# Layer 0 of a four-layer gated cross-attention stack: another path for every second softmax unit

## The reference, cut to what matters

```
q = (emb @ Wq.T).reshape(B, SQ, 16, 64).transpose(0, 2, 1, 3)
k = (context @ Wk.T).reshape(B, SK, 16, 64).transpose(0, 2, 1, 3)
v = (context @ Wv.T).reshape(B, SK, 16, 64).transpose(0, 2, 1, 3)
q = _layernorm(q, qn_w, qn_b)
k = _layernorm(k, kn_w, kn_b)
attn = jnp.einsum('bhqd,bhkd->bhqk', q, k) * scale
attn = jax.nn.softmax(attn, axis=-1)
out = jnp.einsum('bhqk,bhkd->bhqd', attn, v)
return out.reshape(B, SQ, 16 * 64) @ Wu.T + bu      # heads gathered first
x = x + jnp.tanh(g_xattn[0]) * out
```

## Time and profile before

| | |
|---|---|
| median of 3 runs | 1539.65 us (1536.65 to 1540.21) |
| the profiled execution, timed | 1535.79 us |
| its span, first to last instruction | 1533.6 us |
| TensorE busy | 1393.0 us, 91% |
| VectorE busy | 805.6 us, 53% |
| ScalarE busy | 756.1 us, 49% |
| GpSimd busy | 124.2 us, 8% |
| mean granted TensorE clock | 0.978 of full speed |

### The profile page before, as it was taken

How to read it: one execution, slowest core, us unless ns; L and a number is a source line. 1 busy time by engine, 2 the same in 40 slices (tenths; PEclk the granted TensorE clock), 3 DMA queues, 4 the chain that set the end, 5 groups by cost and what they waited for, 6 DMA issues and landing times.

```text
span 1533.6 us, 26446 instructions
## 1 busy us (share of the span) xinstructions
PE 1393.0 (91%) x8788; PEld 1129.2 (74%) x8788; DVE 805.6 (53%) x2147; ACT 756.1 (49%) x1622; POOL 124.2 (8%) x115
## 2 busy tenths in 40 slices
PE   6987899999999987899979888999999998888999
PEld 5685567777898765679947756677779887566898
DVE  4693544554434747753357825445543456476532
ACT  2752455555543454554447425555554434545443
POOL 1042000000000002000011410000000100020000
PEclk9999999999999999999989999999999999999999
DMA  5002000000002000000000020000000020000000
GB/s 199 1 1 111 1 1 1 1 2 1 1 1 93 18 1 1 6 1 15 1 16 1 1 110 1 1 2 1 1 1 2 1 111 1 1 1 1 1 8 8
DMA packets 4038, 27.88 MB, mean 18 GB/s; under 512 B 1054, under 2 KB 1344, under 8 KB 2880
## 3 DMA queue, kind: packets, MB, share of 16 engines
q1 hardware_dynamic: 3184, 22.55, 3.7%
q10 hardware_dynamic: 720, 3.59, 0.6%
HBM read 25.09 MB, written 1.05 MB: 17 GB/s over the span
## 4 chain that ended last, share of the span: by engine, by line
issue 69%; PE 18%; DVE 7%; POOL 3%; ACT 2%; DMA 0%; DVEq 0%; SPq 0%; POOLq 0%; ACTq 0%
PE psum L659 16%; DVE nmax L1345 2%; DVE rsum L1354 1%; POOL rs L1201 1%; PE psum L693 1%; POOL arenaD L1216 1%; ACT arenaB L994 1%; POOL x L1228 1%; DVE arenaA L1572 1%; ACT arenaA L994 1%; DVE xn L1300 1%; DVE psum L1341 0%; DMA mask<-in_mask_dram 0%; DVE x L1377 0%; DVE arenaA L1570 0%
## 5 line engine op out<-in xcount | busy, mean ns | idle before, releaser
L659 PEld LDWEIGHTS psum<-moe,arenaA 128*128 128x128 f32 x2048 | 239.2, 194 | 8.3 <-issue 1.9
L659 PE MATMUL psum<-moe,arenaA 128*128 128x128 f32 x2048 | 241.6, 277 | 2.2 <-DVE gt L1454 1.4
L994 ACT ACTIVATE arenaB<-psum 128x512 f32<-128x512 f32 x448 | 168.2, 428 | 115.7 <-PE psum L693 114.9
L659 PE MATMUL psum<-arenaD,arenaB 128*128 128x128 f32 (+2 forms) x1440 | 190.8, 281 | 13.2 <-ACT arenaB L994 12.6
L994 ACT ACTIVATE arenaA<-psum,vec 128x512 f32<-128x512 f32 (+1 forms) x208 | 125.3, 613 | 156.6 <-PE psum L659 156.4
L659 PEld LDWEIGHTS psum<-arenaD,arenaB 128*128 128x128 f32 (+1 forms) x1440 | 173.7, 193 | 25.6 <-issue 11.2
L1425 DVE CUSTOM_DVE_ANT_0 probs<-psum,shift 128x589 f32<-128x589 f32 x128 | 98.7, 771 | 166.5 <-PE psum L659 164.4
L994 ACT ACTIVATE probs<-probs,nmax 128x589 f32<-128x589 f32 x128 | 100.8, 787 | 170.9 <-DVEq L1428 170.9
L1402 DVE SCALAR_TENSOR_TENSOR x<-psum,gt,x 128x128 f32<-128x128 f32 x256 | 72.0, 344 | 213.7 <-PE psum L659 213.7
L693 PE MATMUL psum<-w_first,probs 128*128 128x128 f32 (+2 forms) x1120 | 160.6, 274 | 8.1 <-POOL probs L1240 3.1
L659 PE MATMUL psum<-parts 128*128 128x512 f32 x672 | 166.4, 397 | 0.0
(11 more groups left out here) (200 smaller groups left out, 1767.6 us busy)
## 6 DMA issues: line engine op xcount, KB each, us to landing
moe<-in_w_moe_dram SPq DMA_DIRECT2D x4, 4096.0 KB, 12.8
moe<-in_w_folds_dram SPq DMA_DIRECT2D x3, 1024.0 KB, 9.7
w_l<-in_w_l_dram ACTq DMA_DIRECT2D x1, 1372.0 KB, 12.7
x<-in_x_dram SPq DMA_DIRECT2D x4, 256.0 KB, 4.0
out_dram<-x SPq DMA_DIRECT2D x4, 256.0 KB, 2.1
w_rest<-in_w_rest_dram ACTq DMA_DIRECT2D x1, 768.0 KB, 8.9
w_first<-in_w_first_dram ACTq DMA_DIRECT2D x1, 596.0 KB, 5.3
w_second<-in_w_second_dram ACTq DMA_DIRECT2D x1, 512.0 KB, 6.6
```

The costliest lines, as they stand in the source:

```text
L659: return nc.tensor.matmul(out, lhsT, rhs, start=start, stop=stop, skip_group_check=shared)
L994: return nc.scalar.activation(out, in_, func, **kw)
```

## The change

On odd units of layer 0 (8 of the 16 of a pair) the maxima are taken off along another path. ScalarE copies the scores from PSUM to the unit's SBUF buffer, which now frees the slot. VectorE takes the maxima from that copy. GpSimd adds the negated maxima, in place, and raises a new signal, `less_ready`. ScalarE's exponential of an odd unit waits for that signal. Even units, and the other layers, keep the old path.

```
+        def by_pool(l, k):
+            return l == 0 and k % 2 == 1
...
 # ScalarE
+            def less_max(l, s, hf, t, i, k):
+                if by_pool(l, k):
+                    act.wait_ge(*filled[i].at("sc", l, s, hf, t))
+                    f(unit_probs[k % 4].rearrange("p (r j) -> p r j", r=2), scores_of(i), ACT.Copy).then_inc(*free[i].mark("sc", l, s, hf, t))
...
-                act.wait_ge(*reader_did("sc", l, s, hf, t))
+                if by_pool(l, k):
+                    act.wait_ge(*less_ready.at(l, s, hf, t))
+                else:
+                    act.wait_ge(*reader_did("sc", l, s, hf, t))
                 f(unit_probs[k % 4], unit_probs[k % 4], ACT.Exp).then_inc(*exp_ready.mark(l, s, hf, t))
...
 # GpSimd
+            def less_max(l, s, hf, t, i, k):
+                if by_pool(l, k):
+                    pool.wait_ge(*unit_max.at(l, s, hf, t))
+                    pr = unit_probs[k % 4].rearrange("p (h k) -> p h k", h=8)
+                    nc.gpsimd.tensor_tensor(pr, pr, nmax[:, k % 4, :].unsqueeze(2).broadcast_to([128, 8, KEYS]), ALU.add)\
+                        .then_inc(*less_ready.mark(l, s, hf, t))
...
 # VectorE
             def less_max(l, s, hf, t, i, k):
-                dve.wait_ge(*filled[i].at("sc", l, s, hf, t))
-                sc = scores_of(i).rearrange("p r (j k) -> p r j k", j=4)
+                if by_pool(l, k):
+                    dve.wait_ge(*reader_did("sc", l, s, hf, t))
+                    sc = unit_probs[k % 4].rearrange("p (h k) -> p h k", h=8)
+                else:
+                    dve.wait_ge(*filled[i].at("sc", l, s, hf, t))
+                    sc = scores_of(i).rearrange("p r (j k) -> p r j k", j=4)
...
-                if not by_head(l, k):
+                if not by_head(l, k) and not by_pool(l, k):
                     dve.wait_ge(*unit_max.at(l, s, hf, t))
```

More of the change, by code:

```diff
@@ L543, in program @@
         unit_max = signal("unit_max")
+        less_ready = signal("less_ready")
         gate_exp = signal("gate_exp")
@@ L1155, in _ @@
             parts = dict(norm_turn=norm_turn, repeat_context=repeat_context, head_norm=head_norm, head_root=head_root,
-                         turn_queries=turn_queries, exp=exp,
+                         turn_queries=turn_queries, exp=exp, less_max=less_max,
                          turn_probs=turn_probs, values0=values0, turn_heads=turn_heads, hidden=hidden, media_turn=media_turn,
@@ L1243, in _ @@
             parts = dict(norm_stats=norm_stats, norm_again=norm_again, media_norm=media_norm, add_bias=add_bias,
-                         normalise=normalise, clear_keys0=clear_keys0, sum_columns=sum_columns, project_heads=project_heads)
+                         normalise=normalise, less_max=less_max, clear_keys0=clear_keys0, sum_columns=sum_columns, project_heads=project_heads)
             pool.memset(half_power[:], -0.5).then_inc(consts_ready.sem, 1)
```

## The result

| | before | changed |
|---|---|---|
| median, runs side by side | 1537.69 us (6 runs) | 1529.91 us (6 runs, 1526.29 to 1532.95) |
| ratio | | 0.9949 (95% interval 0.9931 to 0.9966) |
| all runs of both kernels, the later ones included | median 1536.1, mean 1536.0 (132 runs) | median 1531.1, mean 1531.5 (30 runs) |
| span of the profiled execution | 1533.6 us | 1528.8 us |

The first comparison says 7.8 us faster. Two later ones of the same two kernels say 0.9982 (0.9967 to 0.9996) and 0.9977 (0.9962 to 0.9991). All together the change is worth 4.5 us by the means, give or take 0.6 (one standard error). I forecast 1.4 us, and had called anything under 4.6 us no change.

A forecast was written before the change was run, and what follows sets the result against it. TensorE was taken to bound layer 0's middle periods, so only start and stall counted: -0.7 us a pair, start loss of 1.3 included, -1.4 for two; 1539.65 - 1.4 = 1538.2, given as 1538 us, range 1532 to 1543.5 (8 in 10).

The forecast's parts named there:

- In the middle periods this is 0 on the path: Middle of layer 0: eight VectorE additions fewer a pair, 0.72 us each, gain nothing because TensorE's own work hides it.
- the start: First units of each layer-0 pair: the copy ahead of the table load and later waits put TensorE 1.3 us behind.
- the stall: Iteration 15, TensorE waiting for `xn`: wait shrinks from 6.22 to 4.2 us, net -0.7 us a pair, start loss included.
- first mix: Start of layer 0: TensorE's first mix waits for unit 1's eviction, starting at 87.6 instead of 86.28.
- `ve` starts: VectorE's small 128x4 instruction before `xn` starts at 112.7, then ends with GpSimd's addition of unit 13, 0.7 us earlier.
- TensorE goes on: End of the wait for `xn`: TensorE's transposes start at 118.2 instead of 118.93.
- `ve` behind two GpSimd instructions: Rival at the stall: `ve` also waits for unit 12's product, ending 1.2 us later; +1.0 to +4.4 us in all; chance 0.24.
- The clock stays up: Rival behind the stall: shorter TensorE idle avoids the low clock, saving 3.8 us more, sum -5.2, 1534.4 us; chance 0.12.
- VectorE the bound: Rival for layer 0: VectorE limits after all, 16 additions at 0.72 us give 11.5 us, 1528 us; chance 0.07.
- The eviction behind exp in every period: Rival in layer 0: the start's eviction delay recurs every period, about 1 us per mix, +12 us, 1552 us; chance 0.05.
- The 1.4 us that I had in hand: Middle periods: slack between unit 9's exponential being able to start, 100.3, and unit 7's transposes at 101.08, covering the eviction delay.
- drain of about 1380 ns: Start, after ScalarE's table load: the skill's rule would add 1.4 us of loss; the prediction followed the trace and added nothing.

The follow-up runs named there:

- g5: The kernel before with 113 one-column VectorE memsets added ahead of the loop over pairs; mean 1534.3 us, ratio 0.9990 to before.
- g6: The changed kernel with 15 one-column VectorE memsets added ahead of the loop over pairs; mean 1532.4 us, ratio 0.9975 to before.
- e2: The kernel before with the new path on units 9, 11 and 13 of layer 0 alone; mean 1530.6 us, ratio 0.9952 to before.
- g2: The kernel before with 44 unused TensorE transposes in the wait for `xn` after the layer-0 softmax; mean 1530.2 us, ratio 0.9961 to before.

## Why the prediction was wrong

The forecast was 1538.0 us and the first measurement 1529.9. The 8.1 us between them, by medians, are these:

- **The base, 3.5 us.** I took the change off 1539.65, the median of three runs. The median of 132 is 1536.1. The profiled execution, 1535.79, was nearer, and I had set it aside as 3.9 us fast.
- **The fetches, 1.8 us.** This is the step of the mechanism that failed. "In the middle periods this is 0 on the path" was right, and I let it stand for the whole program outside the start and the stall: the term for all other layers was put at nothing without a reason. I asked what the removed instructions cost, never what their absence moves: 0.9 us per pair in layer 1, shown by g5 and g6.
- **The rest, 1.9 us by medians (1.4 by means),** open, as above.
- **Chance of the first six runs, 1.2 us:** median 1529.9, of all 30 1531.1.

Together they are 8.4 us. Layer 0 gave 0.1 less than forecast, and I had rounded 1538.2 down to 1538, which leaves 8.1. Base and chance, 4.7 us, are the level of the runs and no mechanism: had I started from the profiled execution, the forecast of 1534.4 would still have been 3.3 us above the changed kernel's 1531.1, by the fetches and most of the rest.

The steps in layer 0 held, less 3.26 us:

| step | forecast | measured |
|---|---|---|
| copy 128x616 PSUM to SBUF | 0.72 (0.6 to 1.0) | 0.68 |
| addition on GpSimd | 1.216 (1.2 to 2.4) | 1.216 |
| table load starts | 78.1 | 78.09 |
| transposes of units 0 and 1 | 82.6, 85.05 | 82.59, 85.03 |
| first mix | 87.6 | 87.60 |
| middle period | 5.46 | 5.46 |
| `ve` starts | 112.7 | 112.72 |
| `xn` starts | 116.1 | 116.14 |
| TensorE goes on | 118.2, stall 4.2 | 118.27, stall 4.19 |
| both pairs together | -1.4 | -1.33 |

The rivals. *`ve` behind two GpSimd instructions* (0.24) did not happen, though its condition was met: the product of unit 12 was ready and started at 116.36, and `ve`, 115.98 to 116.43, ended with the addition (115.19 + 1.22 = 116.41), not with the product. So the VectorE instruction that waited was held by the current GpSimd instruction and not by the next one. This agrees with the lock in the Trainium skill ("SBUF — State Buffer", SBUF: two separate sides) and adds who comes next: in all ten traces with unit 13 on the new path, in both pairs, `ve` takes 0.45 us and ends 0.02 to 0.03 us behind the addition. *The clock stays up* (0.12): no, 0.51 and 0.50 behind the stalls. *VectorE the bound* (0.07): no; 1528 would have been near the measured time by a mechanism that isn't there, which the 5.46 us without a bracket exclude. *The eviction behind exp in every period* (0.05): only at the start. The 1.4 us that I had in hand against it later assume that VectorE has caught up; in e2, where it hasn't at unit 9, the step comes back and costs 0.57 us. As for the drain of about 1380 ns that the Trainium skill gives ("ScalarE: Activation LUTs", What ACT_TABLE_LOAD costs), this trace disagrees, and the measurement decides. The load now ends at 81.35 + 1.28 = 82.63 and exp(0) starts at 82.64, nothing between them, as in the earlier trace rows; nor is there a drain ahead of the load, since the copy ends at 80.65 + 0.68 = 81.33 and the load starts at 81.35.

The chances were wrong in one place: all of "faster" stood on mechanisms inside layer 0. For an effect such as the 4.5 us of all runs, just about the bound of 0.3%, I had left 0.14.

## What to carry to other kernels

When instructions leave or join a queue, every later border between its blocks moves, and 15 of them were worth more here (1.8 us) than the edit itself (1.3 us): lay the two traces on each other instruction by instruction, and look for the difference in stretches that the edit doesn't touch. Before crediting an edit, undo its side effect alone: a few fillers ahead of the loop cost nothing and told the two apart. And take the level of a kernel from many runs, while the profile gives the difference: here the first median of before, of three runs, was 3.5 us above that of all 132, while the aligned traces repeat to 0.03.

## What the runs showed of the hardware

- VectorE paused 0.2 to 0.4 us in the same places in each trace of one program, and 0.5 to 0.7 us after it went on a packet of 8192 B of instructions started. Adding 113 instructions did what leaving out 15 does, which fits blocks of 128 instructions (8192 B / 128 = 64 B each). The packet comes after the pause, so what VectorE waits for isn't shown.
- TensorE resting for 4.2 us came back at 1.2 GHz, as it did after 6.2; with 28 to 44 unused transposes in the wait it never did (seven traces, both pairs). One execution of 12 of g2 had a mean clock of 0.936 and took 1544.6 us; why isn't known.
- A stretch of low clock is free where TensorE waits anyway: with and without one at 86 us the stall ended the same, -0.66 and -0.67.
- A small VectorE instruction that waited for a GpSimd one took 0.45 us and ended with it, with another GpSimd instruction ready behind (20 places in ten traces).
